# Two-layer gated cross-attention block on one core: the last keys' products at the beginning of their step, bias products padded to 128 rows, the fifth output product ahead of the last mixed transposes

## The reference

```
x = x + tanh(g_xattn[0]) * L0_xattn(ctx, layernorm(x))   # 8 heads of 64, rotary keys, keys = context + latents (487)
x = x + tanh(g_ffn[0])   * L0_ffn(layernorm(x))          # shared FFN + 8 experts, 2 of them per row
x = x + tanh(g_xattn[1]) * L1_xattn(layernorm(x), ctx)   # 16 heads of 16
x = x + tanh(g_ffn[1])   * L1_ffn(layernorm(x))          # 16 experts of q, k, v mixed per row, causal attention
```

```
up = xf @ up_w + up_b;  hact = gelu(up);  eo = hact @ down_w + down_b
combined = einsum('teh,te->th', eo * 0.1, w)              # w: weights of the 2 chosen experts
shared = (gelu(xf @ sw_up + sb_up) @ sw_down + sb_down) * 0.1
out = (shared + combined) / (max|shared + combined| + 1e-6)
```

## Time and profile before

| what | value |
|---|---|
| median of 3 timed runs | 771.77 us (770.62 to 772.28) |
| the profiled execution's own time | 772.88 us |
| span of the profiled execution | 771.1 us |
| PE busy | 741.3 us, 96% of the span |
| PE weight loads busy | 586.5 us, 76% |
| DVE busy | 459.1 us, 60% |
| ACT busy | 384.1 us, 50% |
| POOL busy | 182.3 us, 24% |
| mean granted TensorE clock | 0.991 |

### The profile page before, as it was taken

The page is one execution under the profiler, slowest core; times in us unless marked ns, Lnnn a source line. Parts: engine busy times, 40 slices in busy tenths (PEclk is TensorE's granted clock), DMA queues, the critical chain, the costliest instruction groups (busy, mean ns, idle before and its releaser), DMA issues.

```text
span 771.1 us, 15004 instructions
## 1 busy us (share of the span) xinstructions
PE 741.3 (96%) x5394; PEld 586.5 (76%) x5394; DVE 459.1 (60%) x1142; ACT 384.1 (50%) x1004; POOL 182.3 (24%) x301
## 2 busy tenths in 40 slices
PE   9999999999998999999999999989999999899997
PEld 8567777777765656899999997666777667889987
DVE  3797877887673330122322324947878887797763
ACT  4676766766664212223233232577787788121130
POOL 3132311212000061000000005754455427311000
PEclk9999999999998989999999999999999999999999
DMA  5432333333210983266565524340000000000001
GB/s 167 104 84 54 87 105 96 109 103 89 69 40 1 319 294 110 70 230 229 186 193 183 174 69 127 97 164 1 3 1 3 2 1 3 0 1 1 1 13 37
DMA packets 43533, 69.77 MB, mean 90 GB/s; under 512 B 6611, under 2 KB 35036, under 8 KB 43204
## 3 DMA queue, kind: packets, MB, share of 16 engines
q1 hardware_dynamic: 41924, 65.14, 27.0%
q0 software_dynamic: 1536, 3.67, 1.6%
HBM read 52.56 MB, written 8.26 MB: 79 GB/s over the span
## 4 chain that ended last, share of the span: by engine, by line
PE 82%; DVE 8%; ACT 4%; issue 3%; DMA 2%; SPq 1%; POOL 0%; ACTq 0%; DVEq 0%
PE ps L1432 12%; PE ps L1690 10%; PE ps L1704 9%; PE ps L1906 7%; PE ps L1494 5%; PE ps L1497 5%; PE ps L1614 4%; PE ps L1536 4%; PE ps L1788 3%; PE ps L1603 3%; PE ps L1556 3%; PE ps L1732 3%; PE ps L1742 2%; PE ps L1507 2%; PE ps L1941 2%
## 5 line engine op out<-in xcount | busy, mean ns | idle before, releaser
L757 ACT ACTIVATE OT<-ps,bt 128x128 f32<-128x128 f32 x168 | 48.0, 368 | 104.4 <-PE ps L1690 103.5
L1432 PE MATMUL ps<-ident,arena 112*122 112x112 f32 (+5 forms) x584 | 82.6, 276 | 7.2 <-ACT rt L799 3.3
L1432 PEld LDWEIGHTS ps<-ident,arena 112*122 112x122 f32 (+5 forms) x584 | 64.1, 155 | 31.2 <-issue 14.9
L969 DVE TENSOR_REDUCE negmax<-ps 112x1 f32<-112x375 f32 x128 | 61.2, 540 | 30.0 <-PE ps L1788 29.9
L1690 PE MATMUL ps<-OT,arena 128*128 128x128 f32 x672 | 78.6, 275 | 0.0
L1906 PE MATMUL ps<-arena_r 128*112 128x384 f32 x384 | 75.8, 345 | 1.9 <-DVE acc L1220 1.0
L1690 PEld LDWEIGHTS ps<-OT,arena 128*128 128x128 f32 x672 | 76.8, 192 | 0.4 <-issue 0.3
L1704 PE MATMUL ps<-arena,OT 128*128 128x256 f32 x336 | 75.8, 379 | 0.0
L1145 DVE COPY yo<-ps 128x256 f32<-128x256 f32 x21 | 8.9, 425 | 103.8 <-PE ps L1704 103.8
L1704 PEld LDWEIGHTS ps<-arena,OT 128*128 128x128 f32 x336 | 62.3, 190 | 7.6
L1906 PEld LDWEIGHTS ps<-arena_r 128*112 128x112 f32 x384 | 63.8, 175 | 4.0 <-DVE arena L1353 1.2
(11 more groups left out here) (281 smaller groups left out, 1447.4 us busy)
## 6 DMA issues: line engine op xcount, KB each, us to landing
arena<-in_up_w SPq DMA_DIRECT2D x21, 1024.0 KB, 5.0
arena<-in_down_w SPq DMA_DIRECT2D x8, 1024.0 KB
arena<-arena SPq DMA_DIRECT2D x128, 60.9 KB, 2.0
arena<-in_wqkv SPq DMA_DIRECT2D x1, 3072.0 KB, 10.4
arena<-in_ctx SPq DMA_DIRECT2D x8, 375.0 KB
slot_rows<-acc SPq DMA_DIRECT2D x6, 448.0 KB, 3.5
OT<-slot_rows SPq DMA_DIRECT2D x21, 128.0 KB, 2.2
slot_out<-yo SPq DMA_DIRECT2D x21, 128.0 KB, 1.7
```

What stands on the lines that cost most here:

```text
L757: act.activation(he[:, i % 2, m, :], ps[:, 2 * (i % 2) + m // 4, (m % 4) * SLOT:(m % 4 + 1) * SLOT], ACT.Gelu, bias=bt[:, i % 3, m:m + 1]) ...
L969: dve.tensor_reduce(negmax[0:TQ, h % 4:h % 4 + 1], ps[0:TQ, S_BANKS[h % 4], 0:TK], AX, ALU.max, negate=True)\
L1432: return pe.transpose(dst, src, ident[0:k, 0:k])
```

## The change

Three edits are made, and each engine that takes part gets its share.

*Last keys.* In step 1 of the last batch, PE makes keys 3 right behind the scores of pair 1, ahead of the product with the values and of the transposes; values 3 stay where they were. ACT copies these keys right behind its first exponential of the step.

*Bias products.* `wT` and `dnb` get 128 rows instead of 9. POOL clears them with two more memsets at the start (128 x 896 and 128 x 256), and ACT writes rows 0 to 8 of `wT`. The products then take all 128 rows, of which 119 are zero. SP waits for the memsets ahead of the first small loads.

*Fifth output product.* PE makes `f_out(4)` behind step 5 of the last small attention, ahead of the last mixed transposes. On DVE `mix_low(7)` stands ahead of `f_out(4)` now and not behind it.

```
-        wT = sb("wT", [E0 + 1, TOK])
+        wT = sb("wT", [P, TOK])
...
-        dnb = sb("dnb", [E0 + 1, D])
+        dnb = sb("dnb", [P, D])
...
+                    if i == 6:
+                        sp.wait_ge(s_fill, N_FILL)
...
+            pool.memset(wT[:, :], 0.0).then_inc(s_fill, 1)
+            pool.memset(dnb[:, :], 0.0).then_inc(s_fill, 1)
             pool.wait_ge(s_fill, N_FILL)
...
                 l0_exp(n, 2 * u)
+                if n == B - 1 and u == 1:
+                    l0_k(n, 3)
...
                 if u < 2:
-                    l0_k(n, u + 2)
+                    if n < B - 1 or u == 0:
+                        l0_k(n, u + 2)
                     l0_v(n, p, u + 2)
...
-            act.activation(wT[:, 0:4 * TQ], ps[0:E0 + 1, 7, 0:4 * TQ], ACT.Copy).then_inc(s_wte, 1)
+            act.activation(wT[0:E0 + 1, 0:4 * TQ], ps[0:E0 + 1, 7, 0:4 * TQ], ACT.Copy).then_inc(s_wte, 1)
...
+            mix_low(7)
             for t in range(4, B):
-                if t == 5:
-                    mix_low(7)
                 f_out(t)
...
                 l0_s(n, p, u)
+                if n == B - 1 and u == 1:
+                    l0_kv(n, p, 3, ("k",))
...
-                if u < 2:
+                if n == B - 1 and u == 1:
+                    l0_kv(n, p, 3, ("v",))
+                elif u < 2:
                     l0_kv(n, p, u + 2)
...
                 f_att(7, 1, g)
-                if g in (1, 2, 4):
-                    f_out((0, 1, 2, 0, 3)[g])
-            for t in range(4, B):
+                if g in (1, 2, 4, 5):
+                    f_out((0, 1, 2, 0, 3, 4)[g])
+            for t in range(5, B):
                 f_out(t)
...
-N_SMALL, N_FILL, N_WARM = 16, 8, 42
+N_SMALL, N_FILL, N_WARM = 16, 10, 42
```

More of the change, by code:

```diff
@@ L745, in _ @@
                     act.wait_ge(s_wt, 2)
-                    act.activation(wT[:, 4 * TQ:], ps[0:E0 + 1, 7, 0:4 * TQ], ACT.Copy).then_inc(s_wte, 1)
+                    act.activation(wT[0:E0 + 1, 4 * TQ:], ps[0:E0 + 1, 7, 0:4 * TQ], ACT.Copy).then_inc(s_wte, 1)
             act.wait_ge(s_down, 2 * FM)
```

## The result

| | before | changed |
|---|---|---|
| median of the 9 executions beside each other | 771.09 us (767.83 to 772.32) | 762.33 us (759.24 to 768.64) |
| ratio, 95% interval | | 0.9897 [0.9873, 0.9922] |
| span of the profiled execution | 771.1 us | 766.8 us |
| mean granted clock in it | 0.991 | 0.989 |

The changed kernel is 1.0% faster. Its executions spread over 9 us, and the profiled one, 768.64 us, is the slowest of the nine. So the profile has to be read piece by piece, not by its span.

The account below looks back on a forecast made before the run. TensorE, busy 96% of the span, was taken as the bound. Gains of 5.0 + 6.05 + 1.7 = 12.75 us gave 759.0 from the 771.77 median; 759.3 was taken, range 757.6 to 764.5.

Parts of the forecast that it names:

- rival (a): Last scores of the first attention: clock falls there all the same, 3.15 us returns, 762.4 us; chance 0.10.
- clock term: Last scores and bias products: both clock falls go, giving back 3.15 and 3.4 us.
- Edit 1, wait: Last batch's keys 3 made earlier: PE idle before the last scores falls from 3.11 to 1.2 us, 1.9 gained.
- rival (c): Sine product's DMA before the last scores: late landing is one execution's whim, time 764.0 us; chance 0.04.
- Edit 2, spacing: Bias products padded to 128 rows: products 0.4325 us apart, saving 1.3 us in the first half, 1.35 in the second.
- The start cost nothing: Program start: two added memsets take about 1.0 us, covered by DVE's idle before the context lands; cost 0.
- rival (b): Bias products: row count doesn't space them, 2.65 us stays; 762.0 us, or 765.4 with the fall; chance 0.07.
- Edit 3: Fifth output product ahead of the last mixed transposes: 1.64 us of PE idle goes, gain 1.7 us.
- No window at 0.50 in the whole span: Sign for the bias products' change: the profile afterwards shows no stretch at 1.2 GHz anywhere.
- the microsecond of idle at 615 us: Second attention: a whole microsecond of PE idle left the clock at 1.00, taken as support for 3.15 us returning.
- Rival (d): Second attention loses its clock, 3.4 us a fall, 772.6 us with four; chance 0.05 with anything else eating the gain.
- Rival (e): Whole kernel: timed runs lack the profile's clock falls, so only 6.25 us is gained, 765.5 us; chance 0.06.

Follow-up runs that it names:

- edit 1 kernel: Kernel before with only the last keys' change (keys 3 and their copy made earlier); 767.93 us, ratio 0.9962.
- grouped kernel: Kernel before with the four nine-row bias products of each half moved behind the four other products, no padding; 766.91 us, ratio 0.9961.
- edit 2 alone: Kernel before with only the bias products padded from 9 to 128 rows; 769.91 us, ratio 0.9984.
- direct test: Kernel before with six idle products on PE ahead of the last scores of the first attention; 771.94 us, ratio 1.0013.

## Why the prediction was right, and where it was not

The forecast was 759.3 us with a range of 757.6 to 764.5. The time is 762.3: inside that range, but above the 757.8 to 761 that the prediction gives for the forecast itself, without rivals. It lies next to the 762.4 of rival (a), which is chance, for the clock did not fall in the place that (a) names. What the rest of this section shows is a sum at full clock that was right, and a clock term that was not.

*Edit 1, wait.* Forecast 1.9 us, from 3.11 to 1.2 of idle; the profiles show 3.11 to 1.16. The mechanism is right in each link: the DMA's wait goes, the cosine product is next to be late, the second exponential is ready just in time. The mean gain is 1.35 ± 0.35, because the late landing of the earlier trace rows is not in every execution: rival (c) was half right in its fact (one of four profiles has 1.43 us of idle, the others 2.6 to 3.1), and not in its conclusion.

*Edit 2, spacing.* Forecast 1.3 + 1.35; the edit 1 kernel, at full clock and unpadded, takes 4.81 and 6.54 us where the changed one takes 3.45 and 5.18: 1.36 + 1.36. The executions say 3.5 ± 0.3 against the before of their job, 3.2 against that of all jobs, so 0.5 to 0.8 of it has no row. The start cost nothing, as said. The row count matters; rival (b) is out, though not for the reason given: what counts is that rows change between products next to each other. The rule of the Trainium skill, TensorE: Matmul & The Clock Gate, section LDWEIGHTS (loading the stationary operand), that only columns count for a load, agrees with the grouped kernel (eight products in 3.73 us, half of them of nine rows). It fails for the order in turn (0.61 against 0.43 us).

*Edit 3.* Forecast 1.7; 1.8 by the rows, 1.4 ± 0.4 by the executions.

*The sum at full clock.* 1.9 + 2.65 + 1.7 = 6.25 forecast, 6.1 measured.

*The clock.* This is the step that failed: 3.15 + 3.4 = 6.55 us were to come back, and 2.4 ± 0.9 did. "No window at 0.50 in the whole span" was not met. Both falls named did vanish from the changed kernel's profiles. Over the 14 profiles:

| place | with the old stretch | with it removed |
|---|---|---|
| before the last scores | 4 falls of 5 (none with 1.43 us of idle) | 0 of 9 |
| bias products (9, 32 or 64 rows in turn with 128) | 3 of 5 | 0 of 9 |
| second attention to begin of the last stage | 9 of 13 | 0 of 1 (idle time filled) |

The third row was missing in the working: the profile of before happened to have no fall there, and the prediction took that (the microsecond of idle at 615 us) as a sign that such idle time does no harm. The same 1.33 us of idle stands in 12 of the 14 profiles: in six of them the clock fell 1.0 to 2.0 us after PE had started again, in the other six, that of before among them, it didn't. Nor are the scores of 64 rows the thinnest work of the kernel, as rival (a) has it: the second attention's scores have 32 rows.

Rival (d) named the place, but took it to be something the change might bring. It was there before: the kernels with edit 1 alone, with edit 2 alone and with PE busier before the last scores have the second attention of before and a fall in it or right behind it. By (d)'s own price one fall gives 759.3 + 3.4 = 762.7, close to what came; it had a chance of 0.05 together with everything else that eats the gain. The kernel before, in 66 executions, never kept its full clock, and lost 5.6 us in the mean, where its profile lost about 6.8. The changed kernel loses 3.2 us in the mean, in its two profiles all of it in the third place, and nothing in 7 of 15 executions, which are then at 759 to 761, the forecast. Rival (e), that the timed executions don't share the profile's falls, was half true.

That idle time brings these falls is supported for the third place. Filling it ended them in all of 5 executions, and more work alone doesn't do it: the same kind of idle products, behind the wait and with the idle time left, didn't hold the clock in 8 of 12. Idle time is not the only condition, since half of the profiles kept the clock behind the same 1.33 us. For the first it rests on the count above, since the direct test failed. For the second place too there is only the count. No long idle time stands there in PE's row, only the spaced-out products; grouping them without padding left no fall in one profile, and that is all that is known. The Trainium skill, same page, section A second HAM failure mode: psum-queue depth-cycling, tells of TensorE losing its clock to frequent short idle times between groups of products. The fall at 607 us agrees with that: 1.33 us of idle stood before it, and no longer idle stretch between 600 us and the fall at 645. Edit 2 alone took one of the three places away and still lost 7.0 ± 1.0 us to the clock, against 5.4 ± 0.5 before; that it gave nothing back stays open.

## What to carry to other kernels

A granted clock in one profile is one draw: read the clock of many executions, split each time into that at full clock and what the clock took, and judge an edit by the first before counting on the second. Pad or group products so that neighbours on TensorE have like row counts; a few rows in turn with 128 cost 0.17 us at each change. When a wait in a chain is shortened, move what is behind it as well (here the cosine product). Filler on TensorE belongs ahead of the wait that is really the late one; here it held the clock only in a kernel that no longer computes the reference, and one that does is still to be run.

## What the runs showed that was not expected

- The cost of a change between row counts is a step: 0.61 us a product with 9, 32 and 64 rows in turn with 128, 0.43 with 96, 112 and 128.
- The kernel before never ran a whole execution at full clock in 66; what the clock took was 1.5 to 14 us.
- A stretch at 1.2 GHz reached 13.6 us in the second attention (607.6 to 621.2), though PE had only 1.33 us of idle ahead of it and hardly any within. With idle products behind the wait it reached 17.1 us (608.26 to 625.32).
- In five executions, idle products of 64 columns, some 0.25 us each, kept the clock up at no measurable price where they lay in idle time, in a kernel with changed results; where they did not lie in idle time, they cost 4.5 us.
